# Feed-forward products of a decoder layer by one level of Strassen over pairs of token groups

## The chip, the cores and the metric

The program runs on one core of a Trainium2 chip. The metric is the device time of one execution in microseconds. The engines are named as the profile names them: PE is TensorE (the matrix engine), PEld its weight loads, DVE VectorE, ACT ScalarE, POOL GpSimd, and SP SyncE, which issues every DMA here.

## The reference, cut

One pre-norm decoder layer in float32 on x of shape 4 x 2048 x 512: a state-space mixer, a cross attention over 77 context rows with 16 heads of 32 channels, and a feed-forward network whose hidden width is 2048.

```python
x = x + attn(layernorm(x))                    # a scan of 4 steps, 8 blocks of 64 channels
x = x + xattn(layernorm(x), ctx)              # Q, K, V: 512 -> 512; 16 heads; softmax over 77 rows; @ Wo.T
h = einsum('bsd,dh->bsh', layernorm(x), W_exp) + b_exp
h = butterfly(h, up_weights)                  # 11 stages, linear in h
h = gelu(h + up_bias)
h = butterfly(h, down_weights)                # 11 stages, linear in h
x = x + einsum('bsh,hd->bsd', h, W_con) + b_con + down_bias
```

Both butterflies are linear, so they can be folded into their neighbours: the feed-forward part is a product with a folded 512 x 2048 matrix, a gelu, and a product with a folded 2048 x 512 matrix.

## The kernel before

**Numbers.** Every large product is made in three passes: each operand is split into a high part of type fp32r and the rest (`hi`, made by ACT with a copy, then `lo`, made by DVE with a subtraction), and `split3` (L354) issues high x high, high x low and low x high into the same PSUM bank (line L360). Each matmul is one weight load (PEld) and one moving pass (PE).

**Stages.** 8192 tokens are taken in 16 groups (`NG`) of 512 (`GT`), a group being 4 tiles (`T`) of 128. Stage 1 (to about 240 us) is the state-space mixer; beside it the two folded feed-forward matrices are made, and stored to DRAM as `wu_scratch` and `wd_scratch`, 16 chunks (`MC`) of 128 x 512 each. Stage 2 is attention, stage 3 the feed-forward network. The result of stage 2 goes to DRAM (`x2_scratch`) and is read again.

**Attention.** `attn_loop` (L333) runs a body 18 times, for g = 0 to 17: two bodies written out, a loop over 12, four written out. Body g makes the scores of group g, the values of group g-1 and part of the output projection of group g-2. On PE (`attn_pe`, L1446) a body is, in order: `turn_p(2)` (transposes of probabilities), `project(2)`, `scores(0)`, `turn_p(3)`, `project(3)`, `scores(1)`, `values(0)` to `values(3)` with the transposes of the next normalized group between them, `turn_p(0)`, `scores(2)`, `project(0)`, `project(1)`, `turn_p(1)`, `scores(3)`, and the four query products of the next group. `scores(t)` uses a key tile that is block diagonal: `kh` and `kl` hold, for each of 4 chunks (`KC`) of 128 channels, 4 heads x 77 = 308 columns (`CK`), with zeros where row and column belong to different heads. One tile of scores is 12 matmuls of 308 columns. DVE takes the maximum, subtracts, and sums (`shift`, `sums`), ACT takes the exponential, POOL divides (`norm`, L659). PSUM banks 4 to 7 go round in 28 slots a body; a slot is free when DVE has read it (`dve_slot`). `values(0)` of body g also waits for the value tiles of its batch (`v_loaded`, L1498).

**SP's order.** Every DMA of attention is issued by SP in one written order (L507 to L535): `turn(g)` stores a finished group and loads the group after next. In bodies 4, 8 and 12, where a new batch begins, SP then issues `load_k` and, once `values` of that body are through, `load_v`, which is 12 small DMAs.

**Feed-forward.** Both folded matrices lie in SBUF, split (`wuh`, `wul`, `wdh`, `wdl`, 16 tiles each). `ffn_pe` (L1566) runs over 16 groups, the middle ones in a loop. A group is 16 chunks m; a chunk is an `up` of 12 matmuls of 512 columns (weights stationary, 512 tokens moving), and 12 matmuls of 512 columns down (128 tokens stationary, 512 output channels moving), which add into the four PSUM banks 0 to 3 through all 16 chunks. Between them ACT takes the gelu and its high part and DVE the low part (`up_hi`, L901; `up_lo`, L1264); `up` runs two chunks ahead, through banks 4 to 7. 16 transposes for the next group stand in the middle. At the end of a group DVE adds the four banks to x2 and SP stores it.

## Time and profile before

| | us |
|---|---|
| median of 3 runs | 2474.61 (2474.15 to 2477.7) |
| the profiled execution, whole | 2468.48 |
| its span | 2466.4 |
| PE busy | 2373.7 (96%) |
| DVE, ACT, POOL busy | 1171.2, 943.5, 466.5 |
| DMA | 141.23 MB, 57 GB/s over the span |

The page is one execution. A matmul's duration in it is its latency, about 390 ns for 512 columns; matmuls overlap, so what a matmul costs is the distance from its start to the next start, which only the timeline gives. Idle time of an engine costs something only where another waits for it; the chain of waits shows where that is.

### The profile page before, as it was taken

What the parts mean: (1) busy time and instruction counts of PE and PEld (TensorE: products, weight loads), DVE (VectorE), ACT (ScalarE), POOL (GpSimd) and SP (SyncE); (2) the same over time, 40 slices, a digit from 0 to 9 for tenths busy, and PEclk for the clock granted to TensorE, in tenths of its full rate; (3) what the DMA queues carried; (4) which work ended last, traced back from release to release, by engine and by line L of the source; (5) the groups of instructions that cost most, each with busy time, mean ns of one, the idle gap of its engine ahead of it and who ended that gap; (6) DMA issues with size and microseconds to landing.
All of it is one profiled execution on the core that took longest, in us unless ns stands there. A gap on an engine that the chain in (4) does not pass through costs nothing.

```text
span 2466.4 us, 32984 instructions
## 1 busy us (share of the span) xinstructions
PE 2373.7 (96%) x11592; PEld 1960.9 (80%) x11592; DVE 1171.2 (47%) x1977; ACT 943.5 (38%) x1504; POOL 466.5 (19%) x554
## 2 busy tenths in 40 slices
PE   8778799999999999999999999999999999999999
PEld 4777578888888887788888888888888888888887
DVE  5999688888888887532222212222222212212211
ACT  3997445444444443433223222223222222323321
POOL 3787222222222222111001001101101101101100
PEclk9988899999999999999999999999999999999999
DMA  9554601101111112400000000000010010000000
GB/s 344 173 186 174 217 1 69 44 34 68 44 53 49 39 52 69 162 1 35 34 15 19 34 19 15 34 34 0 34 34 0 34 34 0 34 34 0 34 17 17
DMA packets 83116, 141.23 MB, mean 57 GB/s; under 512 B 18023, under 2 KB 18535, under 8 KB 82663
## 3 DMA queue, kind: packets, MB, share of 16 engines
q1 hardware_dynamic: 83072, 140.68, 16.4%
q8 instruction: 24, 0.39, 0.1%
q14 instruction: 20, 0.16, 0.0%
HBM read 79.42 MB, written 61.24 MB: 57 GB/s over the span
## 4 chain that ended last, share of the span: by engine, by line
PE 89%; DVE 4%; ACT 3%; POOL 2%; issue 2%; DMA 1%; ACTq 0%; POOLq 0%; SPq 0%; DVEq 0%
PE ps L360 77%; PE ps L1503 5%; PE ps L1483 2%; POOL xu L639 1%; PE ps L1397 1%; ACT tu L770 1%; ACT tu L771 1%; PE ps L1333 1%; PE ps L1416 1%; PE ps L1359 1%; POOL yd L633 0%; DVE ql L1018 0%; DVE xt L1018 0%; DVE es L1196 0%; DVE rmax L1194 0%
## 5 line engine op out<-in xcount | busy, mean ns | idle before, releaser
L1018 DVE TENSOR_TENSOR gtl<-ps,gth 128x512 fp32r<-128x512 f32 x256 | 177.1, 692 | 1089.1 <-ACT gth L907 1089.1
L360 PE MATMUL ps<-xt,wuh 128*128 (+1 forms) x2048 | 638.5, 393 | 5.0 <-DVE xt L1018 4.9
L905 ACT ACTIVATE ps<-ps,up_b 128x512 f32<-128x512 f32 x256 | 169.5, 662 | 990.5 <-PE ps L360 990.5
L360 PEld LDWEIGHTS ps<-xt,wuh 128*128 128x128 f32 x2048 | 383.6, 188 | 93.5 <-DVE xt L1018 8.9
L360 PE MATMUL ps<-wdl,gth 128*128 128x512 f32 x1024 | 402.2, 393 | 0.0
L360 PE MATMUL ps<-wdh,gtl 128*128 128x512 f32 x1024 | 402.1, 393 | 0.0
L360 PE MATMUL ps<-wdh,gth 128*128 128x512 f32 x1024 | 402.0, 393 | 0.0
L360 PE MATMUL ps<-xt,wul 128*128 (+1 forms) x1024 | 400.7, 391 | 0.0
L608 POOL TENSOR_TENSOR rstd<-var_e,mhalf 128x4 f32<-128x4 f32 x48 | 53.2, 1109 | 1300.3 <-DVE var_e L1007 1300.3
L669 POOL TENSOR_TENSOR es<-es,rinv 128x308 f32<-128x308 f32 x256 | 170.9, 699 | 446.3 <-DVE rinv L1207 446.3
L360 PEld LDWEIGHTS ps<-wdh,gth 128*128 128x128 f32 x1024 | 192.2, 188 | 44.1
L360 PEld LDWEIGHTS ps<-wdh,gtl 128*128 128x128 f32 x1024 | 192.1, 188 | 44.1
L360 PEld LDWEIGHTS ps<-wdl,gth 128*128 128x128 f32 x1024 | 192.1, 188 | 43.4
L360 PEld LDWEIGHTS ps<-xt,wul 128*128 128x128 f32 x1024 | 192.3, 188 | 42.5
L907 ACT ACTIVATE gth<-ps 128x512 fp32r<-128x512 f32 x256 | 153.5, 600 | 8.0
L841 ACT ACTIVATE pth<-ps 103x512 fp32r<-103x512 f32 x192 | 101.3, 599 | 108.2 <-PE ps L1483 108.2
L864 ACT ACTIVATE es<-es 128x1232 f32<-128x1232 f32 x64 | 79.0, 1235 | 134.0 <-DVE es L1196 134.0
L1018 DVE TENSOR_TENSOR ptl<-ps,pth 103x512 fp32r<-103x512 f32 x192 | 120.7, 682 | 8.8 <-ACT pth L841 8.7
L1483 PE MATMUL ps<-ident,es 128*103 128x128 f32 x768 | 99.2, 280 | 17.1 <-DVE xt2l L1018 8.1
L1483 PEld LDWEIGHTS ps<-ident,es 128*103 128x103 f32 x768 | 94.2, 174 | 23.7 <-POOL es L669 7.9
L360 PE MATMUL ps<-woh,aoh 128*128 128x512 f32 x256 | 106.2, 415 | 2.8 <-DVE aol L1018 1.4
L360 PE MATMUL ps<-xt2h,wqh 128*128 128x512 f32 x256 | 99.9, 390 | 1.0 <-ACT fold L783 1.0
(186 smaller groups left out, 3753.5 us busy)
## 6 DMA issues: line engine op xcount, KB each, us to landing
x<-x_scratch SPq DMA_DIRECT2D x32, 1024.0 KB, 5.6
xa<-in_x SPq DMA_DIRECT2D x16, 1024.0 KB, 5.4
x_scratch<-xa SPq DMA_DIRECT2D x16, 1024.0 KB, 4.3
x_scratch<-x SPq DMA_DIRECT2D x16, 1024.0 KB, 4.3
out_x<-x SPq DMA_DIRECT2D x16, 1024.0 KB, 4.3
xu<-in_wexpT SPq DMA_DIRECT2D x4, 1024.0 KB, 18.5
yd<-in_wcon SPq DMA_DIRECT2D x4, 1024.0 KB, 9.9
wd_scratch<-fold SPq DMA_DIRECT2D x4, 1024.0 KB, 6.9
```

The source lines that it names most:

```text
L360: mm = pe.matmul(bank, a, b, start=first and i == 0, stop=last and i == n - 1)
L608: nc.gpsimd.tensor_tensor(rstd[:, :], var_e[:, :], mhalf[:, :], ALU.pow).then_inc(ln_pow, 1)
L639: nc.gpsimd.tensor_tensor(xu[:, c, 0:XW], tu[:, d, 2 * o, 0:XW], tu[:, d, 2 * o + 1, 0:XW], ALU.add).then_inc(up_add, 1)
L669: mul = nc.gpsimd.tensor_tensor(e[:, f], e[:, f], r[:, f].unsqueeze(2).broadcast_to([P, HPC, L]), ALU.mult)
L770: A(tu[:, d, 2 * o, 0:XW], xu[:, ca, 0:XW], ACT.Copy, scale=hiw[:, 0, m, q, 2 * o:2 * o + 1]).then_inc(up_mul, 1)
L841: his.done(A(out, bank, ACT.Copy), hi_slot(n))
L864: A(e, e, ACT.Exp, scale=SCALE).then_inc(exp_done, 1)
L905: A(bank, bank, ACT.Gelu, bias=up_b[:, m:m + 1]).then_inc(act_gelu, 1)
L907: A(gth[:, m % 4, :], bank, ACT.Copy).then_inc(act_step, 1)
L1018: sub = lambda o, a, b: V.tensor_tensor(o, a, b.bitcast(F32), ALU.subtract)
L1483: mm = pe.transpose(b[0:KP, j * P:(j + 1) * P], es[t % 2][:, f, c * KP:(c + 1) * KP], ident[:, :])
L1503: mm = pe.matmul(b[0:(c + 2) * HD], v[:, f, V_AT[c]:V_AT[c + 1]], pt[:, 3 * f + c, :], start=(i == 0), stop=(i == len(passes) - 1))
```

## The change

**Strassen.** The 16 groups are taken in 8 pairs (`NP`). For a pair, the product up is a 2 x 2 block product: the blocks of the stationary side are halves of the hidden width and of the input channels, those of the moving side halves of the channels and the two groups. One level of Strassen (the form with 7 products and shared sums) makes 7 products of half-size blocks in place of 8. A unit is one product for one chunk: 56 units up (8 chunks `HC` x 7 `PROD`) and 56 down in a pair. A unit up is 6 matmuls of 512 columns; a unit down is 12 matmuls of 256 columns, since its output block is 256 channels wide.

**Sums.** The sums that the scheme needs are made as follows. Of the weights: POOL (`mix_weights`, `low_weights`) and ACT (`high_weights`) make one chunk's seven blocks, high and low, in each of the 16 attention bodies, and SP stores them to DRAM (`wup_scratch`, `wdn_scratch`). Of the normalized input (`mix_x`) and of the gelu's result (in `pool`'s loop): POOL. Of the products: DVE, from PSUM, five adds of 512 columns a chunk up, and six adds of 1024 columns a pair down (`dn_add`); ACT copies each first product to `U`.

**Streaming.** The weights no longer lie in SBUF. A ring of 7 entries of 2 units (512 KB each) is filled by SP through both halves of every pair, 56 loads a pair. x2 is read twice: once for the statistics, once more late in the pair's down half (`xr_loaded`) for the residual.

**Room.** `kh` and `kl` lose their zeros: they hold 78 columns (`LP`) a chunk. A tile of scores becomes 48 matmuls of 77 or 78 columns over 32 rows, four heads going to four PSUM banks. The freed room holds the weight sums while they are made.

**Loops.** Attention and feed-forward are written out in full; no loop is left there.

The diff, cut to its core:

```diff
@@ attention, PE: scores
-                        mm = split3(pe, ps[:, f, 0:CK], [(qh[:, f, tok], ql[:, f, tok], kh[:, b, f, :], kl[:, b, f, :])])
+                        cols = slice(f * LP, (f + 1) * LP)
+                        for i, (q, k) in enumerate(((qh, kh), (qh, kl), (ql, kh))):
+                            for h in range(HPC):
+                                at = slice(h * HD, (h + 1) * HD)
+                                mm = pe.matmul(ps[:, h, cols], q[at, f, tok], k[at, b, f, :], start=(i == 0), stop=(i == 2))
@@ attention, POOL: norm
+                    if t == 1:
+                        mix_weights(g)
+                    if t == T - 1:
+                        low_weights(g)
@@ attention, ACT: end of the body
+                if g < NG:
+                    high_weights(g)
@@ attention, SP
+            def store_wc(n):
+                sp.wait_ge(wc_lo, n + 1)
...
+                sp.dma_start(to[:, :, 0], raw(wc_h[:, :, :])).then_inc(wc_stored, 16)
+                sp.dma_start(to[:, :, 1], wc_s[:, :, :]).then_inc(wc_stored, 16)
...
+            for g in range(2, NG - 2):
+                b = g // GB
                 turn(g)
+                store_wc(g)
+                load_wc(g + 1)
+                if b and g % GB == 0:
+                    if b < NB - 1:
+                        sp.wait_ge(s_done, T * g)
+                        load_k(b + 1)
+                    sp.wait_ge(pe_slot, SLOTS * g + V_SLOT[-1] + 1)
+                    load_v(b)
@@ feed-forward, SP
+            def load_ring(n):
...
+                if n >= RING:
+                    sp.wait_ge(unit_done, WB * (n - RING) + WB)
+                sp.dma_start(raw(ring[:, n % RING]), d[:, WB * b:WB * (b + 1)]).then_inc(w_loaded[n % RING], 16)
...
+            for p in range(NP):
+                for b in range(UNITS):
+                    if UNITS * p + b + RING < UNITS * NP:
+                        load_ring(UNITS * p + b + RING)
...
+                    if b == UNITS // 2 + 18:
+                        sp.wait_ge(x3_pe, 8 * min(p + 2, NP))
+                        for i in range(2):
+                            sp.dma_start(X[:, i * T:(i + 1) * T, :], x2_g[2 * p + i]).then_inc(xr_loaded, 16)
@@ feed-forward, POOL, second half of a pair
+                if more:
+                    mix_x(p + 1, 0)
+                    mix_x(p + 1, 1)
+                bias(p, 0)
+                if more:
+                    mix_x(p + 1, 2)
+                bias(p, 1)
+                if more:
+                    mix_x(p + 1, 3)
+                add_x(p, 1, 2, 1, DN_22)
+                add_x(p, 1, 2, 0, DN_21)
+                add_x(p, 0, 0, 1, DN_12)
@@ feed-forward, ACT, first half of a pair
+                for c in range(HC):
...
+                    A(U[:, c % 2], ps[:, 4 * (c % 2) + UP_BANK[A11], :], ACT.Copy).then_inc(first_copied, 1)
...
+                    gelu(p, c, Q12, GELU_12, c)
+                    if more and c in (4, 6):
+                        apply3(2 * p + 2 + (c == 6))
+                    if c == HC - 2:
+                        for e in range(GR):
+                            hi_g(p, e)
@@ feed-forward, DVE
+                elif i == DN_11:
+                    dve.wait_ge(xr_ready, 2 * p + 1)
...
+                elif i == DN_21:
+                    dve.wait_ge(x_added, 3 * p + 1)
...
+                    add(G[Q12][c][:, :], b(S4), u2).then_inc(up_sum, 1)
+                    if more and c in (3, 5):
+                        stats3(2 * p + 2 + (c == 5))
...
+                for e in range(GR, UNITS):
+                    lo_g(p, e)
+                    if more and e in (41, 43, 45, 47, 48, 50, 52):
+                        lo_x3(p + 1, SPLIT_ORDER[(41, 43, 45, 47, 48, 50, 52).index(e)])
+                    if e in (19, 27, 43, 46, 51, 55):
+                        dn_add(p, (19, 27, 43, 46, 51, 55).index(e))
@@ feed-forward, PE
+            def up(p, c, j):
+                wh, wl = weights(p, PROD * c + j)
+                if c == 0:
+                    pe.wait_ge(x3_lo, x_split(p, j))
+                if j == A12:
+                    pe.wait_ge(up_sum, summed(p, c, SUM_U2))
...
+            def down(p, e):
+                j, c = divmod(e, HC)
+                wh, wl = weights(p, UNITS + e)
...
+                pe.wait_ge(g_lo, split(p, e))
+                for t in range(T):
+                    tok = slice(t * P, (t + 1) * P)
+                    out = ps[:, DN_BANK[j] + t // 2, t % 2 * HW:(t % 2 + 1) * HW]
+                    mm = split3(pe, out, [(gh[e % GR][:, tok], gl[e % GR][:, tok], wh, wl)],
+                                first=c == 0 and t % 2 == 0 and j in (A11, S2, S3, S1), last=c == HC - 1, go_on=True)
+                mm.then_inc(unit_done, 1)
```

The order of the seven products on PE is A11, S2, S3, A12, S1, A22, S4 (named by the weight-side block), chunk after chunk in the up half, product after product in the down half. A12 adds into the bank that held A11, so it waits until DVE has formed the first sum from that bank's copy and S2 (`SUM_U2`).

## Rows read from the trace of the kernel before

**Rows 1.** Page parts 1 and 4: busy by engine; chain that ended last.

```profile
PE 2373.7 (96%) x11592; PEld 1960.9 (80%) x11592; DVE 1171.2 (47%) x1977; ACT 943.5 (38%) x1504; POOL 466.5 (19%) x554
...
PE 89%; DVE 4%; ACT 3%; POOL 2%; issue 2%; DMA 1%; ACTq 0%; POOLq 0%; SPq 0%; DVEq 0%
```

**Rows 2.** Windows: length; busy (count) PE, PEld, DVE, ACT, POOL; clock, DMA, GB/s.

```profile
338.00:971.00 633.00, 631.10 (x3468) 533.00 (x3467) 541.17 (x770) 286.52 (x448) 167.94 (x254) 1.00 0.15 49
971.00:1012.00 41.00, 35.13 (x175) 28.26 (x174) 24.87 (x43) 16.75 (x29) 6.55 (x10) 0.96 0.44 154
1012.00:2461.00 1449.00, 1443.95 (x6384) 1179.31 (x6383) 323.44 (x576) 412.62 (x660) 101.78 (x95) 1.00 0.07 24
```

**Rows 3.** PE timeline, feed-forward (start us, us, operation): matmuls of 512 columns.

```profile
1500.95 0.39 PE L360 MATMUL ps<-wdh,gth 128*128 128x512 f32 x1
1501.18 0.40 PE L360 MATMUL ps<-wdl,gth 128*128 128x512 f32 x1
```

**Rows 4.** PE timeline, first stage: matmuls of 256 columns.

```profile
119.70 0.28 PE L360 MATMUL ps<-rl,xt1h 128*128 128x256 f32 x1
119.82 0.28 PE L360 MATMUL ps<-rh,xt1l 128*128 128x256 f32 x1
119.94 0.23 PE L360 MATMUL ps<-rh,xt1h 128*128 128x128 f32 x1
```

**Rows 5.** Chain of waits (start, us, what): 32 one-column matmuls with weight loads.

```profile
56.20 3.48 PE ps L1363 x32
```

**Rows 6.** Chain of waits, end of attention body 4 and start of 5.

```profile
475.44 1.70 PE ps L360 x12
...
497.50 0.61 ACT qh L841
...
498.88 4.73 PE ps L360 x24
...
509.37 2.08 PE ps L1503 x9
```

**Rows 7.** Groups by shape (busy us, mean ns | idle before): DVE, ACT, POOL.

```profile
L1018 DVE TENSOR_TENSOR gtl<-ps,gth 128x512 fp32r<-128x512 f32 x256 | 177.1, 692 | 1089.1 <-ACT gth L907 1089.1
...
L1018 DVE TENSOR_TENSOR wql<-wq_raw,wqh 128x2048 fp32r<-128x2048 f32 x1 | 2.3, 2292 | 0.8 <-ACT wqh L801 0.8
...
L905 ACT ACTIVATE ps<-ps,up_b 128x512 f32<-128x512 f32 x256 | 169.5, 662 | 990.5 <-PE ps L360 990.5
L907 ACT ACTIVATE gth<-ps 128x512 fp32r<-128x512 f32 x256 | 153.5, 600 | 8.0
...
L801 ACT ACTIVATE wqh<-wq_raw 128x2048 fp32r<-128x2048 f32 x1 | 1.9, 1942 | 0.0
...
L594 POOL TENSOR_TENSOR wgd<-wgd 128x2048 f32<-128x2048 f32 x1 | 4.1, 4075 | 0.1
...
L594 POOL TENSOR_TENSOR wgd<-wgd 128x1024 f32<-128x1024 f32 x1 | 2.1, 2132 | 0.1
```

**Rows 8.** ACT and DVE timelines: normalization of four tiles, statistics of two.

```profile
596.63 2.92 ACT L702 ACTIVATE xn<-x,nmr,rstd 128x512 f32 x4
...
584.26 1.28 DVE L989 BATCH_NORM_STATS2 st<-x 128x6 f32 x2
```

**Rows 9.** SP's timeline in body 4: issuing the values' loads.

```profile
476.14 2.57 SPq L486 DMA_DIRECT2D vh<-v_scratch  x6
478.76 2.46 SPq L486 DMA_DIRECT2D vl<-v_scratch  x6
```

**Rows 10.** Page part 6, and a window with DMA saturated.

```profile
x<-x_scratch SPq DMA_DIRECT2D x32, 1024.0 KB, 5.6
...
1000.00:1010.00 10.00, 10.00 (x54) 8.52 (x53) 5.93 (x17) 6.30 (x11) 1.21 (x2) 1.00 1.03 365
```

**Rows 11.** PE timeline after its gap, and a window after it.

```profile
983.18 0.54 PE L1483 MATMUL ps<-ident,es 128*103 128x128 f32 x1 [4.13 <-POOL es L669]
...
984.00:987.30 3.30, 3.30 (x15) 3.07 (x15) 1.95 (x3) 1.79 (x3) 0.00 (x0) 0.61 0.00 0
```

More of the change, by code:

```diff
@@ L37, in decoder_layer @@
     CK = HPC * L
+    LP = L + L % 2
     KP = (CK + 2) // 3
@@ L207, in decoder_layer @@
-    w_v = r3.at
-    assert free_es1 >= w_v - 4 * T * D
+    prep = Region(gap_at)
+    wc_s = prep.put("wc_s", [P, PROD, HW], F32)
+    wc_h = prep.put("wc_h", [P, PROD, HW], F32R)
+    assert prep.at <= gap_end
+    r3 = Region(free_first)
+    X = r3.put("X", [P, 2 * T, D], F32)
+    rawx = r3.put("rawx", [P, 4, 2, GT], F32)
+    spots = []
+    for at, end in ((after_keep, after_keep + 4 * T * D), (r3.at, es_end)):
+        while at + 4 * 2 * GT <= end:
+            spots.append(at)
+            at += 4 * 2 * GT
@@ L211, in decoder_layer @@
+    before = spots[-1] + 8 * GT
+    r3 = Region(before + -(-(free_values - before) // (4 * GT)) * 4 * GT)
+    assert r3.at - free_values <= 4 * GT
+    ring_at = r3.at
+    ring = r3.put("ring", [P, RING, WB, 2, HW], F32R)
+    gh = [r3.put(f"gh{i}", [P, GT], F32R) for i in range(GR)]
+    gl = [r3.put(f"gl{i}", [P, GT], F32R) for i in range(GR)]
     places = []
-    for at, end in ((w_early, free_scores), (free_values, free_last2), (free_last, free_values),
-                    (free_last2, nc.sbuf_usable_end), (free_x1, free_first), (w_v, free_last)):
-        while at + 4 * D <= end:
+    for at, end in ((r3.at, nc.sbuf_usable_end), (before, ring_at), (after_keep + 8 * T * D, free_first)):
+        at = -(-at // 32) * 32
+        while at + 4 * GT <= end:
@@ L335, in attn_loop @@
             inside = lambda g: lambda d: 0 <= g + d < NG
-            for g in (0, 1):
-                body(g, inside(g))
-            with eng.Fori(2, NG - 2) as g:
-                body(g, lambda d: True)
-            for g in range(NG - 2, NG + 2):
+            for g in range(NG + 2):
                 body(g, inside(g))
@@ L352, in decoder_layer, with split3 @@
         assert [(h, c) for h, _, _, c, _ in pieces] == [(0, 0), (1, 0), (1, 1), (2, 1), (2, 2), (3, 2)]
-        def split3(pe, bank, parts, first=True, last=True):
+        def split3(pe, bank, parts, first=True, last=True, go_on=False):
             n = 3 * len(parts)
@@ L359, in split3 @@
                 for a, b in ((ah, bh), (ah, bl), (al, bh)):
-                    mm = pe.matmul(bank, a, b, start=first and i == 0, stop=last and i == n - 1)
+                    mm = pe.matmul(bank, a, b, start=first and i == 0, stop=last and i == n - 1, skip_group_check=go_on)
                     i += 1
@@ new lines, in store_wc @@
+            def store_wc(n):
+                sp.wait_ge(wc_lo, n + 1)
+                if n < HC:
+                    to = wup_d[:, PROD * n:PROD * (n + 1)]
+                else:
+                    to = wdn_d.rearrange("p (j k) h n -> p j k h n", k=HC)[:, :, n - HC]
+                sp.dma_start(to[:, :, 0], raw(wc_h[:, :, :])).then_inc(wc_stored, 16)
+                sp.dma_start(to[:, :, 1], wc_s[:, :, :]).then_inc(wc_stored, 16)
+            load_wc(0)
+            for n in range(2):
+                store_wc(n)
+                load_wc(n + 1)
@@ L828, in attn_act @@
                 his.start()
[L829 to L834 removed]
+                if g == NG + 1:
+                    act.wait_ge(x2_stored, 16 * (NG - 2))
+                    act.wait_ge(wc_stored, 32 * NG)
+                    for o in SPLIT_ORDER:
+                        hi_x3(0, o)
                 def hi(out, n):
@@ new lines, in _ @@
+            for p in range(NP):
+                for c in range(HC):
+                    for j in range(PROD):
+                        up(p, c, j)
+                for e in range(UNITS):
+                    down(p, e)
+                    i = e - (HC * 3 + 3)
+                    if p < NP - 1 and 0 <= i < 8:
+                        if i < 2:
+                            pe.wait_ge(up_sum, summed(p, HC - 1, SUM_12))
+                        else:
+                            pe.wait_ge(x3_raw, 8 * (p + 1) + i - 1)
+                        turn3(p + 1, i, 6 + i % 2)
```

587 lines of the change are left out of this document (349 added, 238 removed).

## Prediction

> **What bounds the kernel now.** I read the page's first part, then the chain, then windows by stage. PE is busy for 96% of the span and carries 89% of the chain, DVE 4% [rows 1]: almost every microsecond that PE no longer issues comes off the end, and every one for which it waits is added. The windows place it. In attention's steady part (338 to 971) PE is busy 631 of 633 us at full clock, DVE 541; in the feed-forward part (1012 to 2461) PE 1444 of 1449, DVE only 323, ACT 413, POOL 102, DMA 24 GB/s [rows 2]. So the stage that the change works on is bound by PE's issue alone, and the other engines have room there. A matmul's 390 ns is latency; the price is the distance between starts, 0.23 us for 512 columns [rows 3]. Over the whole stage: 1449 us hold 6144 such matmuls and 240 transposes; at 0.11 us for a transpose (the price of a weight load with a short matmul, 3.48/32 = 0.109, [rows 5]) that leaves (1449 - 26)/6144 = 0.2315 us each.
>
> **Matmuls of the feed-forward part.** Up: 8 pairs x 56 units x 6 = 2688 of 512 columns, x 0.2315 = 622 us. Down: 8 x 56 x 12 = 5376 of 256 columns. The row for that shape, with a new weight load each, shows 0.12 us from start to start [rows 4]: 645 us. Its ends: 0.1157 (half of 0.2315; the weight load alone, 0.109 [rows 5], would not bind) gives 622, and 0.142, what 308 columns cost (1.70/12, [rows 6]), gives 762. Transposes, 7 x 32 x 0.11 = 25 us. Sum 1292 against 1449: a gain of **157 us** (ends 180 and 40). It is less than one eighth of 1449 because 256 columns cost more than half of 512.
>
> **New waits, up half.** PE now depends on DVE within a chunk: A12 may start only when DVE has added S2's bank to ACT's copy of A11. Of the 4.2 us from a chunk's start to A12's turn (A11, S2 and S3 at 6 x 0.2315 = 1.39 each), the sum's two inputs exist after 2.8. In a plain chunk DVE (5 adds of 0.69) and ACT (a copy 0.60 and four gelus 0.66 [rows 7]) are free in time. Where other work stands in front they are not. After chunks 3 and 5 DVE has the statistics of a group, 2 x 1.28 [rows 8] and about 1.0 of small steps behind the last add (0.7), then the sum 0.69: 4.9, late by 0.7. After chunk 4 ACT has add 0.7, gelu 0.66, normalization 2.92 [rows 8], copy 0.6, then DVE 0.69: 5.7, late by 1.5. After chunk 6 four high parts (about 0.53 each) stand there too: 7.8, late by 3.6. Together 0.7 + 1.5 + 0.7 + 3.6 = 6.5 us in each of 7 pairs, 0.7 in the last, 46 us.
>
> **New waits, down half.** A down unit is 12 x 0.12 = 1.44 us. The second read of x2 is issued when unit 37 is done: 2 MB behind 0.5 MB of ring. At 365 GB/s that is 7.1 us and some 2 more to land (1 MB alone lands in 5.6) [rows 10], 9 us. POOL's bias over 2048 columns takes 4.1 (one operation of that size, [rows 7]), DVE's DN_11, two banks wide, about 1.2, the next low part 0.7: 15.1 us, where PE wants unit 47 at 9 x 1.44 = 13.0. Late by 2.1. POOL goes on with 2.1 + 4.1 + 2.1 + 2.1 (1024 columns cost 2.13) before DN_21 may start, and DVE with that and a low part: at 25.7 PE wants unit 52, which with the first delay is 22.3. Late by 3.4. At the pair's end DVE 1.2, POOL 2.1 and ACT's copy stand before the next first sum: late by 0.9. Sum (2.1 + 3.4 + 0.9) x 7 + 2.1 = 47 us. Both halves together 93 us; the ends are 30 (a few tenths sooner at each handover) and 150 (POOL slower beside DVE).
>
> **Attention: the weight sums.** POOL gets about 3.4 + 3.9 us a body beside 633 - 168 of idle time, ACT 1.8 us at the body's end: its last high part ends at 498.1, and PE needs the next bank from it and DVE at 498.88 + 4.73 = 503.6 [rows 6]. I cost these at nothing; if that cover is gone it is 1.8 us x 16.
>
> **Attention: SP's order.** This is what I weigh most. `store_wc(g)` waits for `low_weights(g)`, which ends about 6 us into body g+1 (ACT 1.8, POOL 3.9 from 498.9). Queued behind it are `load_wc`, which waits for the two stores (1.8 MB: 7 us at the rate of [rows 10] with 2 to land, 9 taken because the pieces are 1 KB), and in bodies 4, 8 and 12 `load_k` and `load_v`. The 12 issues of `load_v` take 2.57 + 2.46 us [rows 9], those before them 2, landing 2.5. So the values' tiles, which before were there half a body early, arrive at 498.9 + 6 + 9 + 2 + 5 + 2.5 = 523.4 or a little later, while PE wants them in `values(0)` of body g+1 at 509.4 [rows 6]: 14 to 15 us of idle PE, three times, **44 us** (ends 25 and 60).
>
> **Attention: scores.** 12 matmuls of 308 columns cost 1.70 us a tile [rows 6]; now 48, each with a weight load, in four row groups. No row of before shows two row groups at work. Bounds: if four go side by side, a load at 0.109 for each four is 12 x 0.109 = 1.3 us; if they go one by one, 48 x 0.109 = 5.2 us [rows 5]. Over 64 tiles -25 to +226 us. The nearest row is the serial end, but it reloads the same rows each time, so it can't tell. I take the side-by-side case with some issue cost, 1.7 us, no change, and keep the serial end as a rival.
>
> What the Trainium skill says of it stands apart. "TensorE: Matmul & The Clock Gate", Part 3, says matmuls in different row groups start a few ns apart; no row here shows that. The same page, "LDWEIGHTS", says that a load's time goes by its columns and not its rows, 32 rows costing as much as 128; a load of 128 columns at 0.109 us agrees as far as it goes [rows 5]. Taken alone it speaks against this part: 48 loads for 12. By the first rule the sum stands, by the second without overlap of loads it grows by 226 us.
>
> **Handover, clock, tail.** Between attention and feed-forward the statistics of two groups (7 us on DVE) stand before the last low parts, and the seven split inputs wait for each other through POOL and DVE (4 x 2.1 and 7 x 1.2); stage 3 starts about 13 us later. After PE's gap of 4.13 us the clock of the next stretch is 0.61, a mix of 1.2 and 2.4 GHz [rows 11], costing about 1.7 us. For three gaps of 14 us and half of the seven of 3.6 us I add 14. The last add goes through POOL: 2.5.
>
> **Sum.** 2466.4 - 157 + 93 + 44 + 0 + 13 + 14 + 2.5 = 2476 us of span, 2478 with the 2.1 that lie around it. The profiled run is 6.1 below the median (2468.5 against 2474.6), so I forecast 2483.
>
> **Rivals.** Case A, the sum: **2483**, 38%, own range 2430 to 2545.
> Case B, row groups one by one: every tile of scores 5.2 us, PE still the bound in attention, 2483 + 226 = **2709**, 22%. It adds from 0.035 us a matmul upward (1.70/48), and at 0.087 (1.70 + 157/64 = 4.15 us a tile) it alone outweighs the whole gain. The load's row speaks for it; against it, that the four write different banks and read different rows.
> Case C, faster: half the feed-forward waits are hidden (-46), scores at 1.4 us (-20), and the values come 8 us sooner each time (-24): **2393**, 28%. For it: DVE, ACT and POOL are idle most of that stage, so an order slightly better than my chains hides much. Against it: the orders are strict and the late positions are written in them.
> Case D, the stream: 56 x 512 KB a pair is 29 MB in some 165 us, 178 GB/s on average beside 365 seen at best [rows 10]. If rows of 4 KB, 112 KB apart, or code fetched for unrolled loops bring it below about 180, PE waits for the ring: at 165 GB/s, 8 x 14 = 110 us more than A, less the waits it covers: **2560**, 12%.
>
> **How the numbers follow.** Measurement tells about 0.2% (5 us). Faster: C and a quarter of A, 0.38; same: 0.07; slower: B, D and the rest of A, 0.55. The range goes from C to B, 2385 to 2715; what lies outside is the better half of C and the upper tail of B.
>
> **What the new profile would show.** Down matmuls 0.12 apart; ACT or DVE ending PE's waits before each chunk's A12, longest in chunk 7; DVE's adds with POOL behind them near units 47 and 52; PE idle for 10 us or more before `values(0)` in bodies 5, 9 and 13, ended by a DMA; and the score group's distance: 0.03 or 0.11 us a matmul. The forecast is wrong by most if that last number is not what I took, or if the values' loads are not late.

## The result, and the profile after

Before 2474.4 us, after 2626.5 us (medians; 2473.5 to 2477.7 and 2624.0 to 2629.8): a ratio of 1.061, with a 95% interval of 1.059 to 1.063. The forecast was 2483 with a range of 2385 to 2715, and "slower" was the likeliest sign at 0.55. So the time lies in the range and on the side that had most of the chance, but 143 us above the forecast itself, and above case A's own range (2430 to 2545).

First the page after: busy time by engine, and the shares of the chain that ended last (answers to [rows 1]). PE falls from 96% busy to 88%, and DVE goes from 4% of the chain to 23%.

```profile
PE 2303.6 (88%) x15816; PEld 1993.6 (76%) x15816; DVE 1818.8 (69%) x2433; ACT 1180.8 (45%) x1808; POOL 1114.3 (42%) x914
...
PE 61%; DVE 23%; issue 6%; ACT 5%; DMA 3%; POOL 2%; DVEq 0%; SPq 0%; POOLq 0%; ACTq 0%
```

Then windows, with the columns of [rows 2]: attention with the handover up to the first matmul of the up half, the whole feed-forward part, and one pair of it.

```profile
268.70:1088.90 820.20, 740.38 (x6225) 600.08 (x6226) 640.65 (x890) 364.83 (x541) 317.62 (x390) 0.94 0.30 100
1088.90:2615.60 1526.70, 1349.21 (x8288) 1214.31 (x8288) 947.96 (x1024) 620.13 (x944) 622.98 (x355) 0.95 0.59 184
...
1297.90:1489.10 191.20, 169.52 (x1040) 152.65 (x1040) 116.55 (x130) 78.40 (x120) 77.95 (x45) 0.94 0.59 186
```

The part that was to give 157 us takes 78 more than before (1526.7 against 1449.1), and attention with its handover 74 more (820.2 against 746.1). The granted clock of the feed-forward part was 1.00 and is 0.95. DMA moves 184 GB/s where it moved 24. Last, who ended PE's waits (us in total, times, longest):

```profile
PE ps L402 <- DVE gl L1198: 94.0, 40, 8.4
PE ps L402 <- DVE U L1437: 78.5, 37, 4.0
PE ps L1718 <- issue: 32.6, 3, 12.1
...
PE ps L1698 <- DVE ptl L1198: 18.9, 2, 12.7
```

The first two lines are the feed-forward part's 172 us, the first for low parts in the down half, the second for DVE's sums over the banks, nearly all in the up half. The third is `values(0)` in bodies 5, 9 and 13. No DMA of the ring's stands in the list. The two feed-forward lines don't end on DVE's own work alone; what DVE stood for is read below.

### The profile page after: what moved, and what is told of

It is laid out like the page before. It is cut to its first block, busy times and chain, and to the rows that moved or that the text cites. A ratio compares the mean times of both kernels' runs of the same rounds, so it can differ in the third digit from the quotient of the medians.

```text
span 2624.0 us, 40851 instructions
## 1 busy us (share of the span) xinstructions
PE 2303.6 (88%) x15816; PEld 1993.6 (76%) x15816; DVE 1818.8 (69%) x2433; ACT 1180.8 (45%) x1808; POOL 1114.3 (42%) x914
## 4 chain that ended last, share of the span: by engine, by line
PE 61%; DVE 23%; issue 6%; ACT 5%; DMA 3%; POOL 2%; DVEq 0%; SPq 0%; POOLq 0%; ACTq 0%
PE ps L402 48%; DVE xtl L1198 4%; DVE gl L1198 4%; PE ps L1718 4%; PE ps L1687 2%; DVE ptl L1198 2%; DVE U L1437 2%; DVE st L1169 2%; PE ps L1698 2%; DVE es L1375 2%; ACT X L841 2%; DVE rmax L1373 2%; DVE msum L1181 1%; DMA xa<-in_x 1%; PE ps L1652 1%
## 5 line engine op out<-in xcount | busy, mean ns | idle before, releaser
L402 PE MATMUL ps<-ring,gh 128*128 128x256 f32 x3584 | 686.3, 293 | 94.1 <-DVE gl L1198 94.0
L402 PEld LDWEIGHTS ps<-ring,gh 128*128 128x128 f32 x3584 | 579.9, 199 | 105.9 <-issue 63.4
L402 PE MATMUL ps<-xth,ring 128*128 128x512 f32 x1792 | 576.4, 399 | 85.4 <-DVE U L1437 78.5
L402 PE MATMUL ps<-ring,gl 128*128 128x256 f32 x1792 | 519.7, 290 | 0.0
L1198 DVE TENSOR_TENSOR gl<-G,gh 128x512 fp32r<-128x512 f32 x384 | 403.5, 1075 | 154.5 <-ACT gh L1078 154.1
L402 PEld LDWEIGHTS ps<-xth,ring 128*128 128x128 f32 x1792 | 344.4, 192 | 173.8 <-issue 63.1
L1078 ACT ACTIVATE gh<-G 128x512 fp32r<-128x512 f32 x384 | 239.5, 629 | 287.8 <-PE ps L402 286.5
L402 PEld LDWEIGHTS ps<-ring,gl 128*128 128x128 f32 x1792 | 356.9, 199 | 0.0
L402 PE MATMUL ps<-xtl,ring 128*128 128x512 f32 x896 | 355.7, 397 | 0.0
L402 PEld LDWEIGHTS ps<-xtl,ring 128*128 128x128 f32 x896 | 172.8, 193 | 35.0
```

Of the source, the lines that this page charges most:

```text
L402: mm = pe.matmul(bank, a, b, start=first and i == 0, stop=last and i == n - 1, skip_group_check=go_on)
L1078: A(gh[e % GR][:, :], src, ACT.Copy).then_inc(g_hi, 1)
L1198: sub = lambda o, a, b: V.tensor_tensor(o, a, b.bitcast(F32), ALU.subtract)
```

## The experiments

Eleven kernels ran. Each of e1, e2, e5 and e6 changes one thing in the changed kernel (2626.5); e3 and e7 each make several moves there, all in the order of the up half. e4 takes the scores alone into the kernel before (2474.4). e8 joins several edits, e9 and e11 build on e8, e10 on e9. Every ratio is against the kernel before on the same chip; differences in us are between medians of different chips, on which the kernel before took 2472.4 to 2475.2.

### e1: the values' loads ahead of the weight sums' on SP

```
                 turn(g)
-                store_wc(g)
-                load_wc(g + 1)
                 if b and g % GB == 0:
                     ...
                     load_v(b)
+                store_wc(g)
+                load_wc(g + 1)
```

> Edit: in the changed kernel, SP issues the loads of the next keys and of the values ahead of the store and load of the weight sums, instead of behind them. Theory (queue order): PE's three idle stretches before values(0) in bodies 5, 9 and 13, 32.6 us in all and 9.9 + 8.6 + 7.3 of them on the chain, go, and with them the half clock of 13.65 us after each, which cost up to half of that: 33 + 20 = 53 us less, 2573 us against 2626. Without the clock's part 2593. Rival (the transfers themselves are late, the weight sums share the DMA engines with them): the gaps stay above 5 us each and the time within 10 us of 2626.

Measured: 2589.0 us, ratio 1.046 (1.044 to 1.048), 37 us less. The chain of the changed kernel at this place, and SP's timeline beside it:

```profile
526.47 0.56 DVE x L1364
527.03 9.87 issue
536.90 3.93 PE ps L1718 x9
```

```profile
518.82 0.36 SPq L572 DMA_DIRECT2D wup_scratch<-wc_h  x1
519.22 0.57 SPq L573 DMA_DIRECT2D wup_scratch<-wc_s  x1
527.19 1.18 SPq L564 DMA_DIRECT2D wc_s<-wu_scratch  x2
...
529.75 3.00 SPq L526 DMA_DIRECT2D vh<-v_scratch  x6
532.79 2.46 SPq L526 DMA_DIRECT2D vl<-v_scratch  x6
```

The stores leave at 518.8, the next load may go only when both have landed (527.2), and the last value leaves at 535.2. PE has stood since 524.8, and from 527.0 on this wait is on the chain. With the order turned, body 5 has no such step. The starts of the first softmax step of each body were 58.7, 57.6 and 56.9 us apart where the values were late, 45.6 elsewhere; in e1 all are 45.6. That is 36.2 us for the three, and the whole gain: the queue's order was the cause. Of the 20 us expected for the clock about 4 showed (36.2 us for 32.6 of waits). The trace of the changed kernel says why. The granted clock is 0.50 from 526.8 to 540.4, so the stretch at the lower clock lies mostly within the wait and not behind it, as I had expected: PE stands until 536.9, and only 3.5 us of its work fall into the stretch, 3.7 and 5.1 in bodies 9 and 13. Half of these 12.4 us, some 6, is the most that could come back.

### e2 and e6: POOL's bias left out, and cut into pieces

e2 leaves out most of the output bias, e6 does the same work in other portions.

```
-                tt(xs, xs, ob[:, :].unsqueeze(1).broadcast_to([P, T, D]), ALU.add).then_inc(xr_ready, 1)
+                tt(xs[:, 0, 0:1], xs[:, 0, 0:1], ob[:, 0:1], ALU.add).then_inc(xr_ready, 1)     # e2
+                for t in range(T):                                                              # e6
+                    ins = tt(xs[:, t, :], xs[:, t, :], ob[:, :], ALU.add)
+                ins.then_inc(xr_ready, 1)
```

> Edit: in the changed kernel, POOL's two operations a pair that add the feed-forward output bias to 2048 columns add it to one column only; the rest of that bias is left out of the result. Theory (POOL holds DVE: a DVE operation with two inputs in SBUF stands still while a POOL operation runs, and POOL's 4.5 + 5.0 us delay the sums that free the down banks): DVE's low parts fall from a mean of 1075 ns towards 750, PE's waits for them from 94 us to below 35, the two gaps of 3.6 and 5.4 us a pair go below 1, and with the half clock behind them 8 x (9 + 5) = 110 us go: 2515 us. Rival 1 (the late one is the second read of x, which lands 11 us after its issue): one gap of 3 us or more a pair stays and no more than 40 us go, 2586. Rival 2 (the ring's stream from DRAM holds PE): nothing changes, 2626 within 10.

> Edit: in the changed kernel, each of POOL's two operations a pair that add the output bias to 2048 columns is cut into four of 512 columns; the work is the same. Theory (POOL holds DVE for one instruction at a time, and the wait is for the end of that instruction): DVE's longest low part of 1024 columns falls from 5.57 to under 3 us and PE's gap of 5.4 us a pair to about 3, 8 x 2 to 4 us less with the half clock: 2590 to 2610. Rival 1 (what counts is the sum of DVE's and POOL's time, however it is cut): the same gaps in all, 2626 within 8. Rival 2 (the holds are no lock but slower access for both): every DVE low part beside POOL is longer by the same ratio, and none of the maxima falls.

Measured: e2 2567.8 us, ratio 1.038 (1.036 to 1.040), 59 us less, of which 43 are waits: between the theory (2515) and its first rival (2586), and neither came true as written. PE's waits for low parts fall from 94.0 to 51.0 us (not below 35) and the longest from 8.4 to 2.3 (no gap of 3 us stays). e6: 2628.7 us, ratio 1.063 (1.061 to 1.065), no difference. To see what POOL does to DVE, the timelines of DVE, POOL and PE of the changed kernel in the down half (start us, us, operation, and in brackets the idle time ahead with what ended it):

```profile
1452.78 4.54 POOL L791 TENSOR_TENSOR X<-X,ob 128x2048 f32<-128x2048 f32 x1 [5.95 <-DMA X<-x_scratch]
...
1457.28 2.35 POOL L776 TENSOR_TENSOR rawx<-rawx 128x1024 f32<-128x1024 f32 x1
1457.43 1.22 DVE L1437 TENSOR_TENSOR X<-X,ps 128x1024 f32<-128x1024 f32 x1 [4.84 <-POOL X L791]
1458.57 1.61 DVE L1198 TENSOR_TENSOR gl<-G,gh 128x512 fp32r<-128x512 f32 x1
1459.59 4.99 POOL L791 TENSOR_TENSOR X<-X,ob 128x2048 f32<-128x2048 f32 x1
1460.10 5.57 DVE L1198 TENSOR_TENSOR xtl<-rawx,xth 128x1024 fp32r<-128x1024 f32 x1
1460.23 0.80 PE L402 MATMUL ps<-ring,gh 128*128 128x256 f32 x2 [5.30 <-DVE gl L1198]
1460.83 0.41 PE L402 MATMUL ps<-ring,gl 128*128 128x256 f32 x1
...
1461.47 0.41 PE L402 MATMUL ps<-ring,gl 128*128 128x256 f32 x1
...
1464.54 3.32 POOL L779 TENSOR_TENSOR rawx<-rawx 128x1024 f32<-128x1024 f32 x1
1465.59 2.82 DVE L1198 TENSOR_TENSOR gl<-G,gh 128x512 fp32r<-128x512 f32 x1
...
1468.56 0.76 PE L402 MATMUL ps<-ring,gh 128*128 128x256 f32 x2 [5.40 <-DVE gl L1198]
```

The sum `xtl<-rawx,xth` takes 1.22 us alone and 5.57 here: it begins half a microsecond after POOL's bias and ends 1.1 us (its own work) after it, at 1465.7. The next, 0.69 alone, takes 2.82 behind POOL's next operation. `X<-X,ps`, with one input in PSUM, takes its 1.22 beside POOL as anywhere.

Only the second of the two long waits (5.40 us) is made by this. The first (5.30) is in the main a chain of dependences: the second read of x was issued at 1441.7 and had landed at 1452.8, POOL's bias could start only then, DVE stood 4.84 us for it, and behind it came the sum into X (1.22) and a low part of 1.61 in place of 0.69. e2 takes both away at once, so its 43 us don't part them.

The groups by tile show the exclusion for the whole kernel (ns, shortest/median/longest), first two of the changed kernel, then e6's first:

```profile
L1198 DVE TENSOR_TENSOR xtl<-rawx,xth x56: 1209/1217/5568, 1087.5 to 2432.2; 128x1024 fp32r<-128x1024 f32 x56
...
L1437 DVE TENSOR_TENSOR G<-ps,U x192: 690/691/694, 1108.5 to 2523.4; 128x512 f32<-128x512 f32 x192
```

```profile
L1200 DVE TENSOR_TENSOR xtl<-rawx,xth x56: 1211/2288/3416, 1089.5 to 2437.8; 128x1024 fp32r<-128x1024 f32 x56
```

An input in PSUM: never longer than 694 ns, though POOL works beside these sums. Two inputs in SBUF: up to 5568. With POOL's bias in pieces of 512 columns the longest falls to 3416 and the median rises to 2288: DVE stands for the end of one POOL instruction at a time, not at a ratio. The same holds the other way (a bias operation of e8, below, takes 8.18 us instead of 4.5). PE's waits for low parts were 87.8 us in 51 times for 94.0 in 40, and the kernel's time didn't fall. That smaller portions don't help here is shown; that only the sum of the two engines' times counts, as the rival had it, is not, because the pieces also cost more (a pair's first four took 5.45 us where the whole took 4.54) and the sum into X still waits for all four.

### e3 and e7: the order of the up half

```
# e3: statistics and normalization of the next pair among the first low parts of the down half;
#     the first four high and low parts behind the last chunk's copy and second sum
# e7: ACT
                     A(U[:, c % 2], ps[:, 4 * (c % 2) + UP_BANK[A11], :], ACT.Copy).then_inc(first_copied, 1)
+                    if more and c in (5, 7):
+                        apply3(2 * p + 2 + (c == 7))
...
                     gelu(p, c, Q11, GELU_11, c, ps[:, 4 * (c % 2) + UP_BANK[A12], :])
+                    if c >= HC - GR:
+                        hi_g(p, c - (HC - GR))
# e7: DVE
                     add(u3, b(S3), u2).then_inc(up_sum, 1)
+                    if more and c in (3, 4, 5, 6):
+                        stats3_half(2 * p + 2 + (c > 4), (c - 3) % 2)
```

> Edit: in the changed kernel, the statistics and the normalization of the next pair are moved from between the up half's chunks to the first half of the down half, one tile between two low parts, and the first four high and low parts of the down half stand behind the copy and the sum of the last chunk instead of ahead of them. Theory (strict order on ACT and DVE): PE's gaps before A12 in chunks 4 to 7 (1.64, 1.65, 1.64 and 4.03 us) go, 7 x 9 = 63 us, and the half clock behind the last of them: 63 + up to 40, 2525 to 2565 us. If the moved work makes DVE's low parts late in the down half, it gives some back there: the low parts are to be read for that. Rival (the sum over PE's banks is late by itself, the plain chunks too): the gaps before A12 stay near 1.6 us, and the time within 15 us of 2626.

> Edit: in the changed kernel, the up half's order alone: half a group's statistics behind DVE's second sum in chunks 3 to 6, the normalization behind ACT's copy in chunks 5 and 7, the first four high and low parts of the down half one by one in chunks 4 to 7. The down half is as it was. It splits what the eighth experiment did together. Theory (strict order on ACT and DVE, half clock behind the 4 us gap): PE's waits for DVE's sums over its banks fall from 78 us to about 12, the pair boundaries, and the half clock behind the last chunk goes: 66 + 10 to 25 us less, 2535 to 2550, with the down half's waits at 94 as before. Rival (the up half's gaps only gave the down half time, and come back there): the waits for low parts rise by as much as the others fall.

Measured: e3 2581.4 us, ratio 1.043 (1.041 to 1.045), 45 us less; e7 2549.6 us, ratio 1.031 (1.029 to 1.033), 77 us less. The waits, first of e3, then of e7:

```profile
PE ps L402 <- DVE gl L1208: 120.4, 40, 8.4
...
PE ps L402 <- DVE U L1457: 12.2, 8, 3.2
```

```profile
PE ps L402 <- DVE gl L1197: 86.9, 33, 8.4
...
PE ps L402 <- DVE U L1442: 12.3, 8, 3.3
```

In both, the waits before A12 within a pair are gone, and one of at most 3.3 us a pair is left. In e3 the 4.03 us of chunk 7 came back as a wait for the first low part of the down half (94.0 to 120.4): four high and low parts in a row had only been moved. e7 makes them one by one in earlier chunks, and nothing comes back. Its 73 us of waits are nearly its whole gain, so the clock gave back about 4 us here and not the 10 to 25 that I expected.

### e4: the scores alone, in the kernel before

```
-                        mm = split3(pe, ps[:, f, 0:CK], [(qh[:, f, tok], ql[:, f, tok], kh[:, b, f, :], kl[:, b, f, :])])
+                        cols = slice(f * LP, (f + 1) * LP)
+                        for i, (q, k) in enumerate(((qh, kh), (qh, kl), (ql, kh))):
+                            for h in range(HPC):
+                                at = slice(h * HD, (h + 1) * HD)
+                                mm = pe.matmul(ps[:, h, cols], q[at, f, tok], k[at, b, f, :], start=(i == 0), stop=(i == 2))
```

Attention's loop is written out here too, as in the changed kernel.

> [...] Theory (row groups side by side): 48 in 1.47 us against 12 in 1.70, 64 tiles, 15 us less: 2460 against 2474. Rival 1 (the side-by-side speed holds only where PE waits for DVE anyway): no change, 2474 within 5. Rival 2 (unrolling costs, since PE's instructions are now fetched all through attention): slower by more than 5 us.

Measured: 2473.1 us, ratio 0.9998 (0.9988 to 1.0007). PE's timeline round one group of scores in e4:

```profile
730.60 0.39 PE L358 MATMUL ps<-woh,aol 128*128 128x512 f32 x1
730.92 0.31 PE L1472 MATMUL ps<-kh,qh 32*128 32x78 f32 x4
731.05 0.29 PE L1472 MATMUL ps<-kl,qh 32*128 32x78 f32 x4
...
732.16 0.29 PE L1472 MATMUL ps<-kh,ql 32*128 32x78 f32 x4
732.38 1.56 PE L1483 MATMUL ps<-ident,es 128*103 128x128 f32 x12
```

Four row groups work side by side: four matmuls, each with its weight load, every 0.11 us, 48 in 1.47. But the first stands 0.32 us behind the last of 512 columns instead of 0.23, and the last 0.22 ahead of the next kind. The period of a body fell from 44.45 to 44.19, 0.07 us a tile where 0.23 was expected, and the first two bodies took 4.2 us more (94.1 against 89.9). From 300 to 340 the granted clock (mean of 20 us each) was 0.61 and 0.73 in e4, nearer to the lower of the two levels (1.2 GHz against 2.4), and 0.91 in both in the kernel before. Half of PE's busy time at the lower level in these two bodies, read in windows of 1 us, is 16 us for 6, so the clock is enough for the 4.2. Why it was lower is open. In all: nothing won, nothing lost.

### e5: the weight sums rounded earlier on ACT

```
                 for o in range(KC):
                     hi_q(o)
-                if g < NG:
-                    high_weights(g)
+                    if o == 1 and g < NG:
+                        high_weights(g)
```

> Edit: in the changed kernel, ACT rounds the weight sums (high_weights) after the second high part of the queries instead of after the fourth, at the end of the body. Theory (my cover was gone: the 1.59 us of it stand on the chain between the last high part of the queries and the first one of the next body's turned scores, and POOL's subtraction right behind it holds DVE's msum for 1.72 us): the period of a body falls from 45.63 us to what the scores alone gave beside before, 44.2, and the time by 14 x 1.4 = 20 us, 2606. Rival (the same 1.59 us only meet the third high part of the queries, or POOL's subtraction another sum of DVE): the period stays at 45.6, 2626 within 5.

Measured: 2597.2 us, ratio 1.050 (1.048 to 1.052), 29 us less. The chain at a body's start in the changed kernel:

```profile
512.51 0.60 ACT qh L990
513.11 1.59 ACT wc_h L966
514.69 0.50 ACT pth L990
...
516.42 0.68 DVE ptl L1198
517.10 1.72 DVE msum L1181
```

The 1.59 us stand between the last high part of the queries and the first turned score, and `msum`, a sum of 128x4 with both inputs in SBUF that takes 0.15 us at its shortest, holds the chain for 1.72 while POOL subtracts 1792 columns. Moved, the period of a body falls from 45.63 to 44.2 us, as expected; the first two bodies gave another 7 us, and the three late values were each a little less late (5 us together).

### e8 to e11: the causes together, and who should add the bias

e8 is the edits of e1, e5 and e7, and in the down half an earlier start of the next pair's transposes and splits and of the second read of x:

```
-                    i = e - (HC * 3 + 3)
+                    i = e - 19
...
-                    if b == UNITS // 2 + 18:
+                    if b == UNITS // 2 + 14:
```

> Edit: the changed kernel with the SP order of the first experiment, the early rounding of the weight sums, and another order in the feed-forward part: half a group's statistics behind DVE's second sum in chunks 3 to 6, its normalization behind ACT's copy in chunks 5 and 7, the first four high and low parts of the down half one by one in chunks 4 to 7; in the down half the next pair's transposes and their splits eight units earlier, and the second read of x eight units earlier. Theory (all that is lost is strict order and late starts): 37 + 20 us from attention; in the up half no gap above 0.5 us (63 us and about 30 of half clock); in the down half about half of the 11 us a pair, 50 us with the clock: 2426, between 2390 and 2470. Rival (in the down half DVE and POOL together have more to do than PE, because they can't work at once): gaps of 8 us or more a pair stay there, and the time stays above 2460.

Measured: 2457.4 us, ratio 0.994 (0.992 to 0.996). The edits of e1, e5 and e7 measured singly sum to 144 us; this is 169. By subtraction the down half's own edit gave about 25 to 30 us, half of what the theory asked, and its rival is half right: the time is below its 2460, but a wait of 7.9 us a pair stays. POOL's timeline of e8:

```profile
1530.64 8.18 POOL L791 TENSOR_TENSOR X<-X,ob 128x2048 f32<-128x2048 f32 x1 [5.58 <-DMA X<-x_scratch]
1538.78 2.33 POOL L776 TENSOR_TENSOR rawx<-rawx 128x1024 f32<-128x1024 f32 x1
```

Here POOL is the one that is held, by a row of DVE's low parts and splits, and behind it the mixing that the next split needs is late. The low part for which PE waits 7.9 us had waited 8.46 us for ACT, which is behind that split, and then takes 3.31 us behind POOL's second bias. So the bias was given to PE in e9 (four matmuls a pair of a column of ones against its high and low part, into the banks where A11 and S3 begin) and to DVE in e11.

```
+                    for q in range(2):                                     # e9, PE, at c == 0 of A11 and S3
+                        pe.matmul(ps[:, DN_BANK[j] + q, :].rearrange("p (a n) -> p a n", n=HW), ones[0:33, :],
+                                  v.unsqueeze(1).broadcast_to([33, 2, HW]), start=True, stop=False, skip_group_check=True)
...
+                    if e in (39, 41):                                      # e11, DVE
+                        bias(p, (e - 39) // 2)
```

> Edit: the kernel of the experiment before this one, and the output bias put into PE's banks by four more matmuls of 512 columns a pair (a column of ones against the bias's high and low parts) instead of by POOL over x. The bias of the first product A11 reaches all four quadrants, and the difference of the two halves the two that S3 reaches. PE: 8 x 4 x 0.23 = 7 us more; POOL: 9.5 us a pair less. Theory (POOL's time stands on DVE's in the down half): the down half's gaps fall below 3 us a pair, 25 to 50 us less than with the bias on POOL, 2380 to 2400. Rival (the second read of x was the late one, and is now early enough): no gain, 7 us more than the experiment before.

> Edit: the kernel of the eighth experiment (2457 us, its one long wait a pair is 7.9 us in the down half, with a bias operation of 8.2 us on POOL in front of it), and the two bias additions of 2048 columns given from POOL to DVE, behind its 40th and 42nd low part. Nothing is left out. Theory (DVE and POOL can't work side by side, so the slower of the two should not have the work: 5.0 us each on POOL, about 2.2 each on DVE): the two engines' time together falls by about 5 us a pair, the wait of 7.9 us below 4, and the time by 25 to 50 us, to 2407 to 2432, near the kernel with the bias on PE (2393). Rival (no exclusion, DVE is simply the engine that is full in the down half): 4.4 us a pair are added to the engine that PE waits for, and the time rises by up to 35 us, 2457 to 2492.

Measured: e9 2392.8 us, ratio 0.968 (0.966 to 0.969); e11 2412.4 us, ratio 0.975 (0.973 to 0.977). PE's waits for low parts, of e8, e11 and e9:

```profile
PE ps L402 <- DVE gl L1197: 75.1, 24, 7.9
```

```profile
PE ps L402 <- DVE gl L1190: 36.7, 37, 2.3
...
L1435 DVE TENSOR_TENSOR X<-X,ob x16: 2277/2279/2284, 1184.1 to 2378.4; 128x2048 f32<-128x2048 f32 x16
```

```profile
PE ps L409 <- DVE gl L1202: 14.9, 21, 1.0
...
1032.10:2385.50 1353.40, 1315.86 (x8320) 1183.81 (x8320) 858.08 (x1028) 615.35 (x945) 555.57 (x341) 0.99 0.66 208
```

e11 leaves nothing out and gives 2 x 2.28 us a pair to the very engine that PE waits for, and gains 45 us, because 2 x 5 us leave POOL. If DVE had only been full, the time would have risen, so that rival is out. The gain alone doesn't prove the exclusion: POOL works in order, and with the bias gone its mixings come sooner in any case. How much of the 45 us is shorter holds and how much the shorter queue wasn't measured apart; that the holds exist is shown by the durations above. e9 gained 65 us on e8, more than the 25 to 50 of its theory. It also shows what the scheme can give where the side work doesn't bind: the feed-forward part takes 1353 us against 1449 before, the granted clock is 0.99, and the kernel beats the one before by 3.2%.

e10 takes e9 and moves the statistics of the first two groups behind the last low parts of attention.

```
-                if g == NG - 1:
+                if g == NG:                      # and behind residual(3, -2) of that body
                     stats3(0)
                     stats3(1)
```

> Edit: the kernel with the bias through PE, and the statistics of the first two groups of the feed-forward part taken from the end of attention's last full body to the next body, behind the low parts of the last two tiles' turned scores. Theory (of the 14 us by which the handover got longer, these statistics ahead of the low parts are most: PE waits 12.7 us for them, and POOL's low parts of the last weight sums hold one small step of DVE for 3.85 us): PE's 12.7 us fall below 3, and about 10 us go in all, 2383 against 2393. Rival (the seven split inputs, through POOL and DVE, end the handover anyway): PE waits as much, only later, and the time stays within 3 us of 2393.

Measured: 2393.7 us, ratio 0.968 (0.966 to 0.969), no difference from e9. PE's 12.7 us are gone, and it waits 4.1 us for the softmax's scaling and 8.9 for the normalization instead:

```profile
979.89 1.56 PE L1715 MATMUL ps<-ident,es 128*103 128x128 f32 x12 [0.58 <-POOL es L744]
988.24 2.04 PE L1715 MATMUL ps<-ident,es 128*103 128x128 f32 x8 [4.05 <-POOL es L744]
1007.11 3.22 PE L1669 MATMUL ps<-ident,X 128*128 128x128 f32 x14 [8.90 <-ACT X L843]
```

The rival's time held (the stretch from 976 to 1032 is 56.0 us for 56.1), but not its reason: the new long wait is for the normalization, which follows the moved statistics, and not for the seven split inputs (4.7 us for 5.0). Starting the statistics earlier was not tried.

## Why the prediction was right or wrong

The difference of the profiled spans, 2624.0 - 2466.4 = 157.6 us, by the terms of the sum:

| term | forecast | measured | from |
|---|---|---|---|
| issue of the feed-forward matmuls | -157 | -170 | row spacings, counts |
| waits, up half | 46 | 78 | waits for U; e7 |
| waits, down half | 47 | 94 | waits for gl; e2, e8, e9, e11 |
| clock and rest, feed-forward | part of 14 | 75 | 1526.7 - 1279 - 172.5 |
| values late | 44 | 36 | body starts; e1 |
| weight sums | 0 | 25 | body starts; e5 |
| scores | 0 | -1 (-3 to +2) | e4 |
| handover | 13 | 14 | windows |
| start, tail | 2.5 | 6 | windows |

The row of clock and rest is what the others leave, so that the feed-forward part closes by itself. The wait at a pair's boundary was forecast in the down half's 47 (0.9 a pair) and is measured in the up half's 78. The recorded sums have small slips: its terms give 5.6 and not 5.7 us after chunk 4, 25.4 and not 25.7 before unit 52, and 2484 and not 2483 in the end. None weighs more than 2 us in all.

**Issue: right.** Down matmuls start 0.12 us apart at full clock, as [rows 4] had it, up ones 0.227 (151 in 34.23 us, from 1301.70): 609 + 645 + 25 = 1279 against my 1292.

**Up half: mechanism right, size off.** Chunk 7 has the wait of 3.6 us that I worked out (it is 4.03), from the cause that I gave, four high parts in front of the copy. The others were mis-sized: 0.7 after chunks 3 and 5 and 1.5 after 4 were each 1.64, and the pairs' boundary, taken at 0.9, was 1.28.

**Down half: the step that failed most.** "POOL's bias over 2048 columns takes 4.1" (4.5 at its shortest) and "a low part 0.7" are near what an engine takes alone. I added them as if DVE and POOL could work side by side, and the bound of 150 ("POOL slower beside DVE") was a guess at the right thing without its reason. The first gap came where and as I had it, 5.3 us for 2.1: of the 3.2 more, 2.0 are the second read of x (11.0 us to land for 9; 9.1 to 11.3 in the eight pairs), the rest the bias (4.5 for 4.1) and the held low part (1.61 for 0.7). The second I had before unit 52, behind DVE's DN_21 (3.4 us); there is none there. It stands before unit 48, behind the held split and low part, and is 5.4. The traces show that a DVE operation with both inputs in SBUF and a POOL operation exclude each other. The Trainium skill says this in "SBUF — State Buffer", section "SBUF: two separate sides": the port pair that VectorE and GpSimd share is an exclusive lock, taken for a whole instruction, and a VectorE instruction with two SBUF inputs contends for it with a GpSimd one that reads SBUF. By that rule the traces agree (5.57 us for 1.22, 694 ns at most with a PSUM input, 3.42 with POOL in pieces); it should have been weighed in the prediction. [Rows 7] hold the warning too: before, the low parts were sums from PSUM (`gtl<-ps,gth`), and after they are `gl<-G,gh`, both inputs in SBUF. By the durations of an engine alone, one pair's down half has 52 of these at 0.69 and seven splits at 1.22 on DVE (44 us), and on POOL 16 mixings at 1.3, seven operations of 1024 columns at 2.13 and two of 2048 at 4.5 (45 us). Together that is 89 us, and PE issues for about 84 (56 x 1.44 and the transposes). That comparison is a warning and not the whole cause: POOL still stood idle for 20 us in the middle of that half (from 1417.6 to 1437.9), waiting for its next input, and PE's waits all stand in its last 35 us.

**Clock: the term furthest off in ratio.** I priced three gaps of 14 us and half of the seven of 3.6 us, with 14 us in all. Read in windows of 1 us, the feed-forward part of the changed kernel has 167 us at the lower of the two levels (1.2 against 2.4 GHz), where the kernel before has none, and PE is busy for 108 of them. Half of that, 54 us, is what the clock costs there (an estimate: work at half the clock takes twice as long); the remaining 21 of the 75 are starts and ends that no wait records, and stay open. In e9 the same reading gives 17 us at the lower level and 6 us lost, and in e2 82 and 34. The stretches follow the gaps: from 1458.6 to 1475.7 the clock was at the lower level, between and behind the gaps of 5.3 and 5.4 us, PE worked for 9 us of it, and three matmuls of 256 columns took 0.64 us where they take 0.36. But the price of a gap isn't one number: e1's three, of 9.6 to 12.1 us, gave back 4 us beyond themselves, e7's 73 us of waits also 4, e2's 43 us 16. What counts is how much of PE's work falls into the stretch at the lower level.

**Values: right.** The chain was as written (stores, loads behind them, values last; 519, 527, 535 us); 44 forecast, 36 measured, three times in bodies 5, 9 and 13.

**Weight sums: wrong, with the price named.** I costed them at nothing and wrote that if the cover was gone it was 1.8 x 16 = 29 us. It was gone: the sums cost 25 (18 in the later bodies, 7 in the first two), and e5 gave back 29, of which 5 are the less late values, so that the match with my 29 is partly luck. The step that failed compared ACT's end with the time when PE needs the next bank, but the work behind it is the turned score that DVE and then the values wait for.

**Scores and rivals.** Side by side was right, and so was "no change" (e4). Case B (row groups one by one, 2709) is refuted: 0.03 us a matmul and not 0.11. The Trainium skill ("TensorE: Matmul & The Clock Gate", Part 3) lets matmuls in different row groups start a few ns apart, and e4's rows, four in 0.11 us, agree. Case D (the stream) didn't happen: 184 GB/s, no wait for the ring, and e9 ran at 208. Case C (2393) is not what this order gave, though e9 reached its time: its ground, an order that hides the waits, was sound, but the order had to be made.

So "slower" came partly for the reasons given (strict order, late values). That the time lies in the range is luck: the range reached to 2715 for case B, which didn't happen, and case A's own range ended at 2545. In spans the sum was 148 us short (2624.0 for 2476), in medians 143. About 47 us of it are waits more in the down half and 25 the weight sums in attention, in both of which DVE and POOL hold each other, beside the late read and the added work in the queues; some 61 are more of clock and rest, 32 more in the up half, 3 the small terms, and 21 less for issue and values.

## What to carry to other kernels

When a change turns a sum from PSUM into one with both inputs in SBUF, ask which POOL operations will run beside it, and count the two as if one engine did them; do it for the stretch where the late work stands, and not only for the whole half. If it doesn't fit, giving POOL's work to another engine helped here, even to DVE; cutting it into pieces didn't. A moved group of operations pays only if what is behind it in the queue was the late thing: e7 gained and e3 half returned because the four parts were spread in one and only moved in the other. And two gaps of 5 us close together on PE cost more than themselves: the stretch between and behind them ran at half clock (0.51 from 1460.2 to 1476), which added some 4.5 us to their 10.7.

## What the runs showed of the hardware

- DVE with two SBUF inputs beside POOL: 1.22 us becomes 5.57, 0.69 becomes 2.82 to 5.03; POOL's 4.5 becomes 8.18 in e8 behind a row of DVE's. With one input in PSUM: 690 to 694 ns in 192 of 192.
- Four row groups of 32 rows, 78 columns: 48 matmuls with 48 weight loads in 1.47 us, 0.031 each. But the first stands 0.32 us behind a matmul of 512 columns where 0.23 is usual, and of 0.23 us a tile expected 0.07 were left.
- A matmul of 256 columns with a new load: 0.12 us at full clock, 0.21 in the stretch with the clock at 0.51.
- The granted clock falls within a gap of PE and stays low behind it: 0.50 from 526.8 to 540.4 round a gap from 524.8 to 536.9. In all 167 us of the feed-forward part were at the lower level in the changed kernel, none in the kernel before, 17 in e9.
- The same 2048-column addition: 2.28 us on DVE, 4.5 to 5.3 on POOL. As four matmuls of 512 columns in place of two such additions it is 0.9 us of PE (an estimate, 4 x 0.23).
